# The add that joins the cosine and sine parts of rotary queries and keys: on GpSimd instead of VectorE

## The chip, the cores and the metric

The kernel runs on one core of one Trainium2 chip. The metric is the device time of one execution in microseconds (us). Its engines are TensorE (PE in the profile; PEld is its weight load), VectorE (DVE), ScalarE (ACT), GpSimd (POOL) and SyncE (SP), which starts transfers. Each engine runs its own instructions in program order and waits for the others through counting semaphores.

## The reference

Sixteen sequences of 512 tokens with 512 channels pass through an attention layer and a feed-forward layer. Each layer is wrapped in two layer norms and a residual: `x + layernorm(layer(layernorm(x)))`. What matters here is the attention layer's rotary embedding:

```
q = split_heads(hidden_states @ Wq.T + bq)
k = split_heads(hidden_states @ Wk.T + bk)
apply_rope(x, freqs) = x * cos(freqs) + rotate_half(x) * sin(freqs)
...
scores = einsum('bhqd,bhkd->bhqk', q, k) / sqrt(dh)
weights = softmax(where(causal, scores, -inf))
out = einsum('bhqk,bhkd->bhqd', weights, v)
```

There are 32 heads of 16 channels. The two rotations of the reference (by position and by frame) are one rotation by the summed angle in the kernel's tables.

## The kernel before, in words

The program has two phases: attention for all 16 sequences, then the feed-forward layer for all 16. The change lies in the attention phase. Sequence 0 and the last are written out; sequences 1 to 14 are a loop on every engine.

A sequence is a hand-written order over steps `w`. There are 64 steps (`w` = 0 to 63) that each make one unit of transposed scores on TensorE and its exponentials on ScalarE. Ahead of them lie 16 steps that finish the sequence before. In `w` = 51 to 61 and after the last step each engine also does the **front** of the next sequence: it transposes the normalised input, then projects keys and queries. A front has eight **tiles** `n`, each of 128 tokens by 512 channels: 0 to 3 are keys, 4 to 7 queries. The steps of tile `n` are:

- TensorE projects it into one of two banks of `narrow` (twelve 128x512 matmuls, lines 793 to 795).
- VectorE, `bias_and_cosine` (from line 581): **bias(n)** adds the bias, from PSUM to `biased` (L586), which frees the bank; **cosine(n)** multiplies by the cosine table into `roped` (L590).
- GpSimd, `turn_pairs` (from line 346): two **products** of the swapped halves of `biased` with the sine table, into `turned` (L354 and L356).
- VectorE, `add_sine` (L596): **add(n)**, `roped` = `roped` + `turned`.
- ScalarE, `high_of_k_or_q` (L426): **high(n)** writes the 16-bit high part into `ks` or `qs`.
- VectorE, `low_of_k_or_q` (L603): **low(n)** writes what the high part leaves over.

VectorE's `front` takes them in a staggered order: bias and cosine of `n`, low part of `n - 2`, add of `n - 1`. ScalarE does high(n) two steps after the projection, behind that step's exponentials. `biased` and `turned` have two buffers, `roped` has three. The next sequence's first transposes of queries wait for all eight low parts.

GpSimd has one more duty in these steps. Each key tile of each group of four heads is masked on its diagonal: **mask(k)** (L366, `k` = 0 to 31), in every even step, ahead of that step's `turn_pairs`. TensorE's **weigh(k)** (L896), which multiplies probabilities and values, waits for mask(k). The last ones stand behind the step loop. On GpSimd the order there is tile 6, mask(31), tile 7; on TensorE it is weigh(29), the projection of tile 7, weigh(30), weigh(31), the first parts of the output projection (`project_out`), two transposes (kinds `o` and `a`; **a(3)** is the last), and then the next sequence.

The masks, the products and GpSimd's residual adds (L373) are queued on one engine in one order, so a later one of them can't pass an earlier one.

Of the kernel before, what the change touches and what calls it, by code (L numbers as in the profile page):

```python
# [23 lines left out]
ALU = mybir.AluOpType  # L24
# [7 lines left out]
NT = T // P  # L32
# [38 lines left out]
def attention_phase(nc, x, wT, bias, rope_cos, rope_sin, x1):  # L71
# [5 lines left out]
    with ctx:  # L77
        def sb(name, shape, dt=F32):
            return ctx.enter_context(nc.sbuf_tensor(name, shape, dt))
# [4 lines left out]
        def sem(name):  # L84
            return ctx.enter_context(nc.semaphore(name))
# [30 lines left out]
        turned = sb("turned", [P, 2, C])  # L116
        roped = sb("roped", [P, 3, C])
# [46 lines left out]
        turned_done = sem("turned_done")  # L164
        roped_done = sem("roped_done")
# [134 lines left out]
        @block.sync  # L300
        def _(sp):
            sp.dma_start(xn[:, :, :], x[0, :, :, :]).then_inc(x_in, 16)
            for n in range(4):
                sp.dma_start(probs[:, n, :, :], wT[n]).then_inc(weights_in[n], 16)
            for n in range(4):
                sp.dma_start(bias_sb[:, n, :], bias[n]).then_inc(tables_in, 16)
            sp.dma_start(cos_sb[:, :, :], rope_cos).then_inc(tables_in, 16)
            sp.dma_start(sin_sb[:, :, :], rope_sin).then_inc(tables_in, 16)
            sp.dma_start(xr[:, :, :], x[0, :, :, :]).then_inc(xr_in, 16)

            def sequence(i, last):
                if not last:
                    sp.wait_ge(narrow_full, N_NARROW * i + NC)
                    sp.dma_start(xn[:, :, :], x[i + 1, :, :, :]).then_inc(x_in, 16)
                if not isinstance(i, int) or i > 0:
                    sp.wait_ge(x1_ready, i)
                    sp.dma_start(x1[i - 1, :, :, :], xr[:, :, :]).then_inc(x1_out, 16)
                    sp.wait_ge(x1_out, 16 * i)
                    sp.dma_start(xr[:, :, :], x[i, :, :, :]).then_inc(xr_in, 16)

            sequence(0, False)
            with sp.Fori(1, NB - 1) as i:
                sequence(i, False)
            sequence(NB - 1, True)
            sp.wait_ge(x1_ready, NB)
            sp.dma_start(x1[NB - 1, :, :, :], xr[:, :, :]).then_inc(x1_out, 16)
            sp.wait_ge(x1_out, 16 * NB)

        @block.gpsimd
        def _(pool):  # L330
            nc.gpsimd.memset(ident[:, :], 0.0).then_inc(consts, 1)
            nc.gpsimd.memset(ident16[:, :], 0.0).then_inc(consts, 1)
            nc.gpsimd.memset(causal[:, :], 0.0).then_inc(consts, 1)
            nc.gpsimd.memset(neg_half[:, :], -0.5).then_inc(consts, 1)
            pool.wait_ge(consts, 4)
            for m in (ident, ident16):
                nc.gpsimd.affine_select(out=m[:, :], in_=m[:, :], compare_op=ALU.not_equal, fill=1.0, base=0,
                                        pattern=[[-1, P]], channel_multiplier=1).then_inc(consts, 1)
            tri = causal[:, T - P:T]
            nc.gpsimd.affine_select(out=tri, in_=tri, compare_op=ALU.is_ge, fill=-1e38, base=0,  # L340
                                    pattern=[[-1, P]], channel_multiplier=1).then_inc(consts, 1)
            def inverse_root(i, ready, v, out, done):
                pool.wait_ge(ready, i + 1)
                nc.gpsimd.tensor_tensor(out, v, neg_half[:, :], ALU.pow).then_inc(done, 1)

            def turn_pairs(i, n):

                t = n % NT
                pool.wait_ge(k_and_q_biased, 2 * NT * i + n + 1)
                a = biased[:, n % 2, :].rearrange("p (h d) -> p h d", h=H)  # L350
                o = turned[:, n % 2, :].rearrange("p (h d) -> p h d", h=H)
                s = sin_sb[:, t:t + 1, :]
                half = DH // 2
                nc.gpsimd.tensor_tensor(o[:, :, 0:half], a[:, :, half:DH],  # L354
                                        s[:, :, 0:half].broadcast_to([P, H, half]), ALU.mult)
                nc.gpsimd.tensor_tensor(o[:, :, half:DH], a[:, :, 0:half],  # L356
                                        s[:, :, half:DH].broadcast_to([P, H, half]), ALU.mult).then_inc(turned_done, 1)

            def mask(i, n):

                kt = n % NT
                exps_done = held(pool, NS * i + 2 * n + 2)
                pool.wait_ge(consts, 7)
                pool.wait_ge(st_read, exps_done)
                d = probs[:, kt, :, P * kt:P * kt + P]
                nc.gpsimd.affine_select(out=d, in_=d, compare_op=ALU.is_ge, fill=0.0, base=0,  # L366
                                        pattern=[[0, HG], [1, P]], channel_multiplier=-1).then_inc(masked, 1)

            def residual(i, t):
                if t == 0:  # L370
                    pool.wait_ge(xr_in, 16 * (i + 1))
                pool.wait_ge(projected_normed, NT * i + t + 1)
                added = nc.gpsimd.tensor_tensor(xr[:, t, :], xr[:, t, :], attn[:, t, :], ALU.add)  # L373
                if t == NT - 1:
                    added.then_inc(x1_ready, 1)

            def sequence(i, last):
                for w in range(2, NS + 1):
                    if w == PROJECTED_AT[NT + 1] + 1 and (not isinstance(i, int) or i > 0):
                        inverse_root(i - 1, var1_ready, var1[:, :], rstd1[:, :], rstd1_ready)  # L380
                    if (not isinstance(i, int) or i > 0) and w in RESIDUAL_AT:
                        residual(i - 1, RESIDUAL_AT.index(w))
                    if w % 2 == 0:
                        mask(i, w // 2 - 1)
                    if not last and w == VARIANCE_AT + 3:
                        inverse_root(i + 1, var_ready, var[:, :], rstd[:, :], rstd_ready)
                    n = w - FRONT_AT - NC - 1
                    if not last and 0 <= n < FRONT_SLOTS - NC:
                        turn_pairs(i + 1, n)
                if not last:  # L390
                    for n in range(FRONT_SLOTS - NC, 2 * NT):
                        turn_pairs(i + 1, n)

            inverse_root(0, var_ready, var[:, :], rstd[:, :], rstd_ready)

            for operand in (ks, qs, vs):
                nc.gpsimd.memset(operand[:, :, :, :], 0.0).then_inc(padding, 1)
            pool.wait_ge(padding, 3)
            nc.gpsimd.memset(ks[:, :, :, 3 * DH:3 * DH + 2], SHIFT_UNIT).then_inc(padding, 1)
            nc.gpsimd.memset(vs[:, :, :, DH:DH + 1], 1.0).then_inc(padding, 1)  # L400
            pool.wait_ge(largest_ready, 1)
            nc.gpsimd.partition_all_reduce(largest_all[:, :], largest[:, 0:4], P, RMAX).then_inc(largest_reduced, 1)
            for n in range(2 * NT):
                turn_pairs(0, n)
            sequence(0, False)
            with pool.Fori(1, NB - 1) as i:
                sequence(i, False)
            sequence(NB - 1, True)
            inverse_root(NB - 1, var1_ready, var1[:, :], rstd1[:, :], rstd1_ready)
            for t in range(NT):  # L410
                residual(NB - 1, t)
# [85 lines left out]
        def _(dve):  # L497
# [93 lines left out]
                                        cos_sb[:, t:t + 1, :].broadcast_to([P, H, DH]),  # L591
                                        ALU.mult).then_inc(k_and_q_biased, 1)

            def add_sine(i, n):
                dve.wait_ge(turned_done, 2 * NT * i + n + 1)
                nc.vector.tensor_tensor(roped[:, n % 3, :], roped[:, n % 3, :], turned[:, n % 2, :],  # L596
                                        ALU.add).then_inc(roped_done, 1)

            def low_of_k_or_q(i, n):
                t = n % NT  # L600
                dst, at = (ks, 2 * DH) if n < NT else (qs, DH)
# [5 lines left out]
            def front(i, f):  # L607

                n = f - NC
                if 1 <= f <= NC:  # L610
                    low_of_x(i, f - 1)
                if n < 0:
                    return
                if n < 2 * NT:
                    bias_and_cosine(i, n)
                if n >= 2:
                    low_of_k_or_q(i, n - 2)
                if n == NT:

                    nc.vector.memset(qs[:, :, :, 3 * DH:3 * DH + 2], 0.0)  # L620
                if 1 <= n <= 2 * NT:
                    add_sine(i, n - 1)

            def bias_v(i, t):
                dve.wait_ge(v_full, NT * i + t + 1)
# [782 lines left out]
```

## Time and profile before

| | us |
|---|---|
| runs shown, median (lowest to highest of three) | 3414.96 (3407.57 to 3424.21) |
| the profiled execution, span from first to last instruction | 3413.7 |
| TensorE busy | 2990.8 |
| VectorE busy | 2466.5 |
| ScalarE busy | 1692.8 |
| GpSimd busy | 759.4 |

The page gives the profiled execution by its span. A busy time includes time in which an instruction has been started and is held up, so an operation that looks long may have been waiting. In a row of the timeline the first number is the start in us from the span's start, the second the duration; in brackets stands the idle time before it and what ended it. A wait that ends for several reasons is put down to the last.

### The profile page before, as it was taken

The page shows a single profiled execution, that of the slowest core. Times are in us where ns is not written, and L with a number is a line of the kernel's source. Part 1 is how long each engine was busy: PE and PEld are TensorE (multiplying, and loading weights), DVE is VectorE, ACT ScalarE, POOL GpSimd, SP SyncE. Part 2 cuts the span into 40 slices and gives each one's busy share as a digit, 9 for nine tenths or more (in the row PEclk, how much of TensorE's full clock was granted, in tenths as well). Part 3 has the DMA queues.
Part 4 walks back from the last instruction along what each step waited for, and adds up shares of the span by engine and source line. Part 5 has one row for each costly group of instructions (what it writes and reads, how often), then busy time and mean ns, then how long its engine had stood idle before and what let it go on. Part 6 is the DMA issues. An engine that isn't in the chain of part 4 may idle for free. (4 is left out here: it accounts for less than half of the span.)

```text
span 3413.7 us, 65137 instructions
## 1 busy us (share of the span) xinstructions
PE 2990.8 (88%) x19840; PEld 1439.9 (42%) x19840; DVE 2466.5 (72%) x7030; ACT 1692.8 (50%) x2220; POOL 759.4 (22%) x918
## 2 busy tenths in 40 slices
PE   3798998988889888888888888897299999999998
PEld 1344444444444444444444444443144444444443
DVE  8778778787887878878788787885655545455554
ACT  1647475574755647566475664755322222222222
POOL 3132332323323223332233322332000000000000
PEclk9999999999999999999999999999599999999999
DMA  2000010000100001000010000000311111111110
GB/s 99 1 13 28 12 38 27 14 26 14 38 27 14 26 14 38 26 14 26 14 38 26 14 26 14 26 26 14 142 38 49 61 49 55 44 51 60 49 61 37
DMA packets 16419, 118.72 MB, mean 35 GB/s; under 512 B 2304, under 2 KB 2304, under 8 KB 2944
## 3 DMA queue, kind: packets, MB, share of 16 engines
q1 hardware_dynamic: 16128, 114.90, 8.9%
q8 instruction: 175, 2.87, 0.4%
q14 instruction: 116, 0.95, 0.1%
HBM read 81.34 MB, written 33.55 MB: 34 GB/s over the span
## 5 line engine op out<-in xcount | busy, mean ns | idle before, releaser
L452 ACT ACTIVATE probs<-ring,exp_scale 128x1024 f32<-128x1024 f32 (+3 forms) x1024 | 811.9, 798 | 339.5 <-PE ring L882 334.5
L641 DVE CUSTOM_DVE_ANT_0 narrow<-narrow,causal 128x384 f32<-128x384 f32 (+3 forms) x1760 | 816.6, 487 | 105.8 <-PE narrow L866 102.1
L866 PE MATMUL narrow<-kTz,qT 128*128 128x384 f16 (+3 forms) x1760 | 502.7, 299 | 158.2 <-DVE row_max L641 126.9
L366 POOL TENSOR_SCALAR_AFFINE_SELECT probs<-probs 128x512 f32<-128x512 f32 x512 | 326.6, 638 | 1361.3 <-ACT probs L452 1360.6
L882 PE MATMUL ring<-qmT,kTz 128*128 128x512 f16 (+3 forms) x2048 | 449.3, 301 | 1.7 <-ACT probs L452 1.0
L1262 DVE SCALAR_TENSOR_TENSOR hidden<-gu,up_scale,silu 128x512 f32<-128x512 f32 x176 | 132.0, 750 | 419.2 <-PE gu L1312 419.2
L1121 ACT ACTIVATE silu<-gu,gate_scale 128x512 f32<-128x512 f32 x176 | 121.0, 688 | 632.2 <-PE gu L1312 632.2
L866 PEld LDWEIGHTS narrow<-kTz,qT 128*128 128x128 f16 x1760 | 170.8, 97 | 545.8 <-DVE row_max L641 459.4
L896 PE MATMUL av<-probs,vs 128*32 128x512 f32 (+3 forms) x4096 | 379.3, 445 | 1.4 <-ACT oT L457 0.6
L1310 PE MATMUL gu<-f_xT_hi,gate_hi 128*128 128x512 f16 x704 | 267.9, 381 | 52.1 <-issue 52.1
L641 DVE DVE_READ_ACCUMULATOR2_ANT row_max<- 128x1 f32 x2048 | 284.7, 139 | 0.0
L1312 PE MATMUL gu<-f_xT_lo,gate_hi 128*128 128x512 f16 x704 | 267.8, 380 | 0.0
L1310 PE MATMUL gu<-f_xT_hi,up_hi 128*128 128x512 f16 x704 | 267.6, 380 | 0.0
L1312 PE MATMUL gu<-f_xT_lo,up_hi 128*128 128x512 f16 x704 | 267.6, 380 | 0.0
L1324 PE MATMUL down<-down_hi,hid_hi 128*128 128x512 f16 x704 | 266.8, 379 | 0.2 <-DVE hid_lo L1273 0.2
L1328 PE MATMUL down<-down_hi,hid_lo 128*128 128x512 f16 x704 | 266.8, 379 | 0.0
L1096 POOL TENSOR_TENSOR f_rstd<-f_var,f_neg_half 128x4 f32<-128x4 f32 x32 | 32.3, 1009 | 930.3 <-DVE f_var L1239 647.6
L793 PE MATMUL narrow<-w_hi,xT_hi 128*128 128x512 f16 x512 | 195.6, 382 | 47.5 <-DVE xT_lo L573 47.5
L882 PEld LDWEIGHTS ring<-qmT,kTz 128*128 128x128 f16 x2048 | 180.8, 98 | 85.6 <-issue 24.5
L444 ACT ACTIVATE kTz<-turn 64x1024 f16<-64x1024 f16 x128 | 130.4, 1019 | 152.0 <-PE turn L839 149.7
L444 ACT ACTIVATE qT<-turn 128x1024 f16<-128x1024 f16 x128 | 130.6, 1020 | 131.0 <-PE turn L839 131.0
L794 PE MATMUL narrow<-w_lo,xT_hi 128*128 128x512 f16 x512 | 194.8, 380 | 0.0
(159 smaller groups left out, 5225.7 us busy)
## 6 DMA issues: line engine op xcount, KB each, us to landing
xn<-x SPq DMA_DIRECT2D x16, 1024.0 KB, 4.8
xr<-x SPq DMA_DIRECT2D x16, 1024.0 KB, 4.8
x<-xr SPq DMA_DIRECT2D x16, 1024.0 KB, 3.9
f_xn<-x SPq DMA_DIRECT2D x16, 1024.0 KB, 4.8
f_xr<-x SPq DMA_DIRECT2D x16, 1024.0 KB, 4.8
out<-f_xr SPq DMA_DIRECT2D x16, 1024.0 KB, 3.9
raw_gate<-gateT SPq DMA_DIRECT2D x1, 2816.0 KB, 10.9
raw_up<-upT SPq DMA_DIRECT2D x1, 2816.0 KB, 17.4
```

Of the source, the lines that this page charges most:

```text
L366: nc.gpsimd.affine_select(out=d, in_=d, compare_op=ALU.is_ge, fill=0.0, base=0, pattern=[[0, HG], [1, P]], channel_multiplier=-1).then_inc ...
L444: nc.scalar.activation(dst, src, ACT.Copy).then_inc(turn_read_act, 1)
L452: nc.scalar.activation(probs[:, kt, 2 * pair:2 * pair + 2, P * kt:T], transposed_scores_at(w), ACT.Exp, scale=exp_scale[:, 0:1]).then_inc( ...
L641: nc.vector.tensor_tensor_reduce(out=bank[:, 0:n], in0=bank[:, 0:n], in1=causal[:, T - n:T], scale=1.0, scalar=-3e38, op0=ALU.add, op1=ALU ...
L793: nc.tensor.matmul(out, a_hi, b_hi, start=first, stop=False)
L866: nc.tensor.matmul(bank_of_maximum(2 * s + j)[:, 0:P * (qt + 1)], qT[:, g % 2, pair, P * qt:P * (qt + 1)], kTz[j][:, g % 3, pair, 0:P * (q ...
L882: last = nc.tensor.matmul(transposed_scores_at(w)[:, j, :], kTz[j][:, g % 3, pair, P * kt:P * (kt + 1)], qmT[:, g % 2, pair, P * kt:T], st ...
L896: last = nc.tensor.matmul(av[32 * j:32 * j + 32, P * kt:T], vs[:, kt, HG * g + j, :], probs[:, kt, j, P * kt:T], start=kt == 0, stop=kt == ...
L1310: nc.tensor.matmul(gu[:, bank, :], hi[:, c, cols], xT_hi[:, c, :], start=c == 0, stop=False)
L1312: last = nc.tensor.matmul(gu[:, bank, :], hi[:, c, cols], xT_lo[:, c, :], start=False, stop=end and not with_rest)
L1324: nc.tensor.matmul(down[:, t, :], hid_hi[:, b % 3, rows], down_hi[:, b, :], start=b == 0, stop=False)
L1328: last = nc.tensor.matmul(down[:, t, :], hid_lo[:, b % 3, rows], down_hi[:, b, :], start=False, stop=b == NI - 1)
```

## The change

GpSimd makes the add itself, directly behind the two products of the same tile, and signals `roped_done`; before it, it waits on its own semaphore until the second product has been written. VectorE's `add_sine` and its call are removed.

```diff
@@ turn_pairs, GpSimd
                 nc.gpsimd.tensor_tensor(o[:, :, half:DH], a[:, :, 0:half],
                                         s[:, :, half:DH].broadcast_to([P, H, half]), ALU.mult).then_inc(turned_done, 1)
+                pool.wait_ge(turned_done, 2 * NT * i + n + 1)
+                nc.gpsimd.tensor_tensor(roped[:, n % 3, :], roped[:, n % 3, :], turned[:, n % 2, :],
+                                        ALU.add).then_inc(roped_done, 1)
@@ VectorE
-            def add_sine(i, n):
-                dve.wait_ge(turned_done, 2 * NT * i + n + 1)
-                nc.vector.tensor_tensor(roped[:, n % 3, :], roped[:, n % 3, :], turned[:, n % 2, :],
-                                        ALU.add).then_inc(roped_done, 1)
...
                     nc.vector.memset(qs[:, :, :, 3 * DH:3 * DH + 2], 0.0)
-                if 1 <= n <= 2 * NT:
-                    add_sine(i, n - 1)
```

The order of GpSimd at the end of sequence 0, from tile 5 to tile 7 of the next front, was (the selects are mask(30) and mask(31)):

```order
L354 TENSOR_TENSOR turned<-biased,sin_sb 128x32x8
L356 TENSOR_TENSOR turned<-biased,sin_sb 128x32x8
L366 AFFINE_SELECT probs<-probs 128x4x128
L354 TENSOR_TENSOR turned<-biased,sin_sb 128x32x8
L356 TENSOR_TENSOR turned<-biased,sin_sb 128x32x8
L366 AFFINE_SELECT probs<-probs 128x4x128
L354 TENSOR_TENSOR turned<-biased,sin_sb 128x32x8
L356 TENSOR_TENSOR turned<-biased,sin_sb 128x32x8
```

In the changed kernel the same place reads:

```order
L354 TENSOR_TENSOR turned<-biased,sin_sb 128x32x8
L356 TENSOR_TENSOR turned<-biased,sin_sb 128x32x8
L359 TENSOR_TENSOR roped<-roped,turned 128x512
L369 AFFINE_SELECT probs<-probs 128x4x128
L354 TENSOR_TENSOR turned<-biased,sin_sb 128x32x8
L356 TENSOR_TENSOR turned<-biased,sin_sb 128x32x8
L359 TENSOR_TENSOR roped<-roped,turned 128x512
L369 AFFINE_SELECT probs<-probs 128x4x128
L354 TENSOR_TENSOR turned<-biased,sin_sb 128x32x8
L356 TENSOR_TENSOR turned<-biased,sin_sb 128x32x8
L359 TENSOR_TENSOR roped<-roped,turned 128x512
```

One add now stands ahead of each of the two last masks, and all adds before them stand ahead of both. On VectorE the steps of two tiles in the middle of the same front were (low part, add, bias, cosine, and again):

```order
L603 TENSOR_TENSOR ks<-roped,ks 128x32x16
L596 TENSOR_TENSOR roped<-roped,turned 128x512
L586 TENSOR_TENSOR biased<-narrow,bias_sb 128x512
L590 TENSOR_TENSOR roped<-biased,cos_sb 128x512
L603 TENSOR_TENSOR ks<-roped,ks 128x32x16
L596 TENSOR_TENSOR roped<-roped,turned 128x512
```

and are now:

```order
L601 TENSOR_TENSOR ks<-roped,ks 128x32x16
L589 TENSOR_TENSOR biased<-narrow,bias_sb 128x512
L593 TENSOR_TENSOR roped<-biased,cos_sb 128x512
L601 TENSOR_TENSOR ks<-roped,ks 128x32x16
```

VectorE keeps three steps per tile, in the order they had. TensorE's and ScalarE's orders are as before.

## Rows read from the trace of the kernel before

**Rows 1.** The page, busy us with share of the span and instructions, by engine.

```profile
PE 2990.8 (88%) x19840; PEld 1439.9 (42%) x19840; DVE 2466.5 (72%) x7030; ACT 1692.8 (50%) x2220; POOL 759.4 (22%) x918
```

**Rows 2.** Windows: us, busy PE, PEld, DVE, ACT, POOL, clock, DMA share, GB/s.

```profile
200.00:230.00 30.00, 30.00 (x185) 13.26 (x184) 24.49 (x37) 14.63 (x18) 18.93 (x20) 1.00 0.02 7
```

**Rows 3.** Timeline of VectorE, one front: start, us, instruction, idle time before it.

```profile
495.57 0.69 DVE L596 TENSOR_TENSOR roped<-roped,turned 128x512 f32<-128x512 f32 x1
...
497.26 0.69 DVE L586 TENSOR_TENSOR biased<-narrow,bias_sb 128x512 f32<-128x512 f32 x1 [1.00 <-PE narrow L795]
...
509.38 0.69 DVE L603 TENSOR_TENSOR ks<-roped,ks 128x512 f16<-128x512 f32 x1
509.98 1.21 DVE L596 TENSOR_TENSOR roped<-roped,turned 128x512 f32<-128x512 f32 x1
...
511.83 1.08 DVE L590 TENSOR_TENSOR roped<-biased,cos_sb 128x512 f32<-128x512 f32 x1
...
515.57 0.69 DVE L586 TENSOR_TENSOR biased<-narrow,bias_sb 128x512 f32<-128x512 f32 x1 [0.30 <-PE narrow L795]
```

**Rows 4.** Line 366, the masks: who waited for it (us in all, times).

```profile
  PEld av L896: 8.4, 33
```

**Rows 5.** Timeline of GpSimd, the front before's first product and this front.

```profile
345.47 0.72 POOL L354 TENSOR_TENSOR turned<-biased,sin_sb 128x256 f32<-128x256 f32 x1 [4.02 <-DVE roped L590]
...
491.83 0.72 POOL L354 TENSOR_TENSOR turned<-biased,sin_sb 128x256 f32<-128x256 f32 x1 [4.03 <-DVE roped L590]
...
497.48 0.63 POOL L366 TENSOR_SCALAR_AFFINE_SELECT probs<-probs 128x512 f32<-128x512 f32 x1
...
509.54 1.10 POOL L354 TENSOR_TENSOR turned<-biased,sin_sb 128x256 f32<-128x256 f32 x1 [0.83 <-DVE roped L590]
510.61 1.17 POOL L356 TENSOR_TENSOR turned<-biased,sin_sb 128x256 f32<-128x256 f32 x1
511.74 0.63 POOL L366 TENSOR_SCALAR_AFFINE_SELECT probs<-probs 128x512 f32<-128x512 f32 x1
...
514.06 1.17 POOL L356 TENSOR_TENSOR turned<-biased,sin_sb 128x256 f32<-128x256 f32 x1
515.19 0.63 POOL L366 TENSOR_SCALAR_AFFINE_SELECT probs<-probs 128x512 f32<-128x512 f32 x1
```

**Rows 6.** Timeline of TensorE's weight loads, weigh(31).

```profile
515.87 0.18 PEld L896 LDWEIGHTS av<-probs,vs 128*32 128x32 f32 x8 [0.25 <-POOL probs L366]
```

**Rows 7.** Timeline of TensorE, first matmul of the next sequence in the loop.

```profile
523.34 0.38 PE L793 MATMUL ring<-w_hi,aT_hi 128*128 128x512 f16 x1 [2.15 <-issue]
```

**Rows 8.** Groups by line, VectorE's add: count, busy us, mean ns, idle us before.

```profile
L596 DVE TENSOR_TENSOR roped<-roped,turned 128x512 f32<-128x512 f32 x128 | 135.6, 1059 | 0.0
```

**Rows 9.** Timeline of GpSimd, residual adds of another sequence: a pair, then one alone.

```profile
274.67 2.84 POOL L373 TENSOR_TENSOR xr<-xr,attn 128x512 f32<-128x512 f32 x2
...
278.07 1.27 POOL L373 TENSOR_TENSOR xr<-xr,attn 128x512 f32<-128x512 f32 x1
```

**Rows 10.** Timeline of GpSimd in the set-up: waits on its own semaphores.

```profile
2.15 0.55 POOL L337 TENSOR_SCALAR_AFFINE_SELECT ident<-ident 128x128 f32<-128x128 f32 x2 [0.49 <-POOL neg_half L334]
...
23.66 3.51 POOL L397 MEMSET vs<- 128x4096 f32 x1
27.23 0.48 POOL L399 MEMSET ks<- 128x256 f16 x1
```

**Rows 11.** Timeline of the set-up: first product of tile 0, first transposes of queries.

```profile
67.48 0.72 POOL L354 TENSOR_TENSOR turned<-biased,sin_sb 128x256 f32<-128x256 f32 x1 [21.33 <-DVE roped L590]
...
93.94 1.03 PE L839 MATMUL turn<-ident,qs 128*128 128x128 f16 x8 [9.88 <-DVE qs L603]
```

**Rows 12.** Windows behind the set-up's projections, columns as in rows 2.

```profile
84.00:89.00 5.00, 0.07 (x1) 0.00 (x0) 4.93 (x8) 1.69 (x2) 3.35 (x4) 1.00 0.00 0
89.00:90.00 1.00, 0.00 (x0) 0.00 (x0) 0.65 (x1) 0.31 (x1) 1.00 (x2) 0.61 0.00 0
...
102.00:103.00 1.00, 1.00 (x4) 0.40 (x3) 0.80 (x4) 0.00 (x0) 0.00 (x0) 0.57 0.00 0
```

## The prediction

> **What bounds the kernel now.** I read the busy shares first, to see which engine has no slack: TensorE is busy 88% of the span, GpSimd (POOL) 22% [rows 1]. That is an average, so I went to the stretch where the change acts, the front of the next sequence inside the attention phase. In a 30 us stretch there TensorE is busy 30.00 us, VectorE (DVE) 24.49, GpSimd 18.93 [rows 2]. TensorE sets the pace and VectorE follows it: bias(7) began only when TensorE's projection was done, after 0.30 us of waiting [rows 3]. Freeing VectorE in a stretch that TensorE fills earns nothing by itself.
>
> Next I looked for where TensorE waits for GpSimd. Over the whole run it is 8.4 us in 33 waits [rows 4], which looks like nothing. The place matters, though. At the end of a sequence TensorE runs weigh(30) and weigh(31), each needing its mask. mask(31) starts at 515.19, takes 0.63 and ends at 515.82 [rows 5]; weigh(31)'s weight load starts at 515.87, and its wait was ended by that mask [rows 6]. So **mask(31) has no slack at all**, and it is already queued on GpSimd right behind the products of tile 6, which start at 514.06 and take 1.17 [rows 5]. Behind weigh(31) TensorE goes on without a gap through project_out and the transposes to the sequence's end; then come 2.15 us of issue time at the loop's branch and the next sequence [rows 7]. Every microsecond that mask(31) slips is a microsecond per sequence.
>
> **What the change removes.** 128 adds on VectorE, 135.6 us, 1059 ns on average [rows 8]. Alone such an add takes 0.69 (the first one of this front, 495.57); inside the stretch it takes 1.21 [rows 3], since it waits for GpSimd, as shown next. VectorE's three other steps keep their durations or get longer, and its cosine is ready no earlier where TensorE's projection is what it waits for. I cost this removal at 0: what covers it is TensorE's own work, 30.00 of 30 us.
>
> **How the two engines share.** A product alone takes 0.72 (491.83); beside VectorE 1.10 or 1.17 [rows 5]. Take tile 5: low(3) runs on VectorE from 509.38 to 510.07 [rows 3]; the first product is issued at 509.54 and ends at 510.64 [rows 5], which is 0.72 after 509.92, shortly before low(3) ends. add(4), issued at 509.98, ends at 511.19, which is 0.69 after 510.50; the second product, issued at 510.61, ends at 511.78. So an operation of GpSimd and a VectorE operation with both inputs in SBUF take turns: whichever comes second begins about 0.13 before the other's recorded end. The mask does it too: cosine(6), issued at 511.83 beside mask(30), takes 1.08 instead of 0.69 [rows 3, 5]. The bias step, with an input in PSUM, shows no such wait.
>
> **What it adds on GpSimd.** One 128x512 f32 add per tile. The same form stands in the trace as the residual: 1.27 alone, 1.42 each in a pair beside VectorE [rows 9]. I take 1.27, because I add the turns separately. The GPSIMD Engine Reference of the Trainium skill, section on elementwise cycle accounting, gives 2.6 cycles an element at 1.2 GHz; an estimate from that is 1.11 us and a total of about 3455 to 3467, and its advice to leave elementwise work to VectorE speaks against this change. The row of 1.27 decides. The add also waits for the second product through a semaphore of GpSimd's own. The trace has such waits at 0.06 (a memset ending at 27.17, the next at 27.23) and 0.49 (before the select at 2.15) [rows 10]; I take 0.1, as the first is in warmed-up code, and keep both as ends.
>
> **The queue of one sequence, step by step.** Until add(1) GpSimd has gaps and swallows the new work; add(1) ends near 498.5, where mask(28) began at 497.48 before [rows 5]. From there on it is busy without a break:
> - tiles 2 to 6: 0.72 + 0.72 + 0.1 + 1.27, less 0.06 of overlap between instructions, is 2.75 each, five times 13.8 us;
> - masks 28 to 31: 0.60 each with the overlap, 2.4 us;
> - one real gap of 0.6 us, when cosine(3) itself waited for add(2);
> - turns: VectorE runs cosines 2 to 6 and low parts 0 to 5 in this time, eleven operations, each waited out once. Before, such a wait cost 0.38 and 0.45 (1.10 and 1.17 less 0.72); with 0.42 it is 4.6 us.
>
> Sum 21.4 us, so mask(31) ends near 519.9 instead of 515.82. The mask before it slips to about 515.7, only 0.1 beyond what TensorE asks for. TensorE's shift is 519.9 - 515.8, **about 4.0 us per sequence** after rounding. The adds themselves come no later than VectorE needs them: add(7) ends near 522.7, and high(7) in ScalarE's queue stands behind a transpose that has itself slipped to about 525. There are 15 such tails (sequence 15 prepares no successor): 15 x 4.0 = 60 us.
>
> Once, in the set-up, all eight tiles run with nothing else: GpSimd starts at 67.48, TensorE gets its first transposed queries at 93.94 [rows 11]. Now the tiles follow each other at 2.75 plus two turns of 0.42, 3.6 us: 67.5 + 0.6 + 2.75 + 7 x 3.55 = 95.7 less the overlaps, say 95.2, plus high 1.06 and low 0.69 and hand-overs is 97: **3 us**.
>
> Sum: 3413.7 + 60 + 3 = 3477 us. The span of the profiled execution is 1.3 us below the median of the runs shown, 3414.96, so both can be used alike.
>
> **Bounds.** The same queue with the add at 1.27 to 1.42 [rows 9] and the self-wait at 0.06 to 0.49 [rows 10] gives 3.8 to 5.8 us per tail, so 3474 to 3504. Downwards the turns are the unknown: if GpSimd gets the shared path more often than VectorE and loses 0.2 instead of 0.42 each, the tail costs 4.0 - 2.4 = 1.6 us, in all 3413.7 + 24 + 3 = 3441. The range is 3444 to 3506.
>
> **The rivals.**
> - *No turns for the add (not slower).* If the add runs beside VectorE without waits on either side, a tile costs GpSimd 2.75 us and half a mask, about 3.05, against 3.7 from TensorE (bias(2) at 497.26 and bias(7) at 515.57 both waited for it, five tiles apart [rows 3]); no lag builds up, and mask(31) still ends at about 515.8. The point that decides is whether it ends by 515.87. Time 3414 to 3417. For it: the GpSimd share of 22% [rows 1]. Against it: every product and every cosine that met the other engine was held [rows 3, 5]. Advanced Engine Details and Errata of the Trainium skill, section on VectorE performance modes, says GpSimd and two-port VectorE instructions block each other and lists no two-port mode for tensor_tensor; by that alone this rival would hold, and the 1.21 against 0.69 shows that two SBUF inputs are enough. Chance 0.06.
> - *VectorE was the hidden bound (faster).* Before the tail, in tiles 4 to 6, VectorE's rows follow each other without idle time [rows 3]. If TensorE's next bank waited on that chain, an add of 1.06 us would come back in each: 3 x 1.06 x 15 = 48 us, 3366. TensorE's 30.00 of 30 us [rows 2] leaves no room for it. Chance 0.03.
> - *The clock falls in the stall (much slower).* In the set-up TensorE idled from about 84.1; its granted clock was 1.00 until 89 and 0.61 in the microsecond after it, so it fell near 89.2 from 2.4 to 1.2 GHz, and it was back only at about 102.9 [rows 12], nine microseconds after work resumed at 93.94 [rows 11]. That idle time was ten microseconds, the stall forecast here is four, and the 2.15 us at the loop's branch cost no clock; the trace has nothing between. If the clock fell in every tail, up to half of nine microseconds would come on top: 15 x 4.5 = 67 us, about 3545. Chance 0.06.
> - *The change doesn't do what it says* can be left out: the order shows the add moved.
>
> **How the numbers follow.** The forecast has 0.85, most of it inside 3444 to 3506. A measurement of this kernel tells from no change about 0.5%, 17 us, so the line for slower is 3432 and for faster 3398. The forecast and the clock rival are slower (0.91), less 0.01 for very small waits; the first rival is the same (0.06, with that 0.01); the second is faster (0.03).
>
> **What would show it.** Right: in the changed profile mask(31) ends about 4 us after the products of tile 6 would have let it, weigh(31) waits some 3.5 to 4 us for the mask at each of 15 tails (TensorE's wait for the mask grows from 8.4 to about 65 us), the period of a sequence grows from 146.4 (345.47 to 491.83 [rows 5]) to about 150.4 us, the new add takes 1.27 to 1.7 with its turns, and the projections before the tail start at the same distance from each other as now. Wrong: masks on time and a period of 146; or GpSimd on time and TensorE waiting for the low parts at the next sequence's first transposes instead; or a granted clock below 1.00 behind the stall.

## The result and the profile after

The changed kernel took **3518.39 us**, the median of 4 runs (3511.66 to 3526.54), beside 3412.17 for the kernel before in the same series (4 runs, 3407.57 to 3424.21): a ratio of 1.031, 95% interval 1.0283 to 1.0337. The forecast had the direction and missed the size: 3518 lies above its range. Of the 106 us between the two kernels it accounted for 63.

First the queue, since the forecast worked it out instruction by instruction. GpSimd in the changed kernel, from a front's first product to the mask that TensorE waits for; start, us, instruction, idle time before it:

```profile
504.22 0.72 POOL L354 TENSOR_TENSOR turned<-biased,sin_sb 128x256 f32<-128x256 f32 x1 [4.03 <-DVE roped L593]
...
510.83 1.09 POOL L369 TENSOR_SCALAR_AFFINE_SELECT probs<-probs 128x512 f32<-128x512 f32 x1
...
527.28 0.63 POOL L369 TENSOR_SCALAR_AFFINE_SELECT probs<-probs 128x512 f32<-128x512 f32 x1
527.88 0.73 POOL L354 TENSOR_TENSOR turned<-biased,sin_sb 128x256 f32<-128x256 f32 x1
528.56 0.72 POOL L356 TENSOR_TENSOR turned<-biased,sin_sb 128x256 f32<-128x256 f32 x1
529.36 1.59 POOL L359 TENSOR_TENSOR roped<-roped,turned 128x512 f32<-128x512 f32 x1
530.91 1.09 POOL L369 TENSOR_SCALAR_AFFINE_SELECT probs<-probs 128x512 f32<-128x512 f32 x1
```

The front begins 12.39 us later than the one in [rows 5] (504.22 against 491.83), so mask(31) would have ended at 528.21 with the old queue. It ends at 532.00: **3.8 us late**, where the forecast said 4.0. The add begins 0.08 after the second product's end (528.56 + 0.72, then 529.36); 0.1 was taken.

TensorE at the same place, columns alike:

```profile
527.96 0.64 PE L892 MATMUL av<-probs,vs 128*32 128x256 f32 x8
532.05 0.43 PE L892 MATMUL av<-probs,vs 128*32 128x128 f32 x8 [3.45 <-POOL probs L369]
...
539.94 0.38 PE L789 MATMUL ring<-w_hi,aT_hi 128*128 128x512 f16 x1 [2.60 <-issue]
...
540.59 0.63 PE L789 MATMUL ring<-w_hi,aT_hi 128*128 128x512 f16 x1
...
541.87 0.63 PE L789 MATMUL ring<-w_hi,aT_hi 128*128 128x512 f16 x1
...
544.00 0.38 PE L789 MATMUL ring<-w_hi,aT_hi 128*128 128x512 f16 x1
```

weigh(31) waits 3.45 us; the forecast was 3.5 to 4. The wait is not quite all that a tail loses. The first matmul of project_out stands here, in the kernel before and in the changed one:

```profile
516.25 0.39 PE L793 MATMUL ring<-w_hi,aT_hi 128*128 128x512 f16 x1
...
532.41 0.39 PE L789 MATMUL ring<-w_hi,aT_hi 128*128 128x512 f16 x1
```

From the front's first product that is 24.42 and 28.19 us. TensorE goes on 3.77 us later, by the whole shift of the mask; 15 tails make 56.5 us.

But behind the loop's branch (in [rows 7] the same place) a matmul of the same form takes 0.63 instead of 0.38 for 3.4 us. The windows show why; columns as in [rows 2], two more windows being from 30 us later:

```profile
535.00:540.00 5.00, 2.40 (x14) 1.28 (x13) 2.66 (x5) 1.54 (x2) 0.00 (x0) 1.00 0.02 3
540.00:544.00 4.00, 4.00 (x17) 1.99 (x18) 0.00 (x0) 0.00 (x0) 0.00 (x0) 0.57 0.04 8
...
566.00:571.00 5.00, 3.42 (x15) 1.09 (x13) 3.72 (x13) 1.43 (x2) 0.00 (x0) 1.00 0.01 2
571.00:575.00 4.00, 3.11 (x18) 1.94 (x19) 3.43 (x16) 2.90 (x4) 0.63 (x1) 0.57 0.02 4
```

The granted clock is 0.57 in two stretches of four microseconds, that is, 3.4 us at 1.2 GHz and the rest at 2.4. I call such a stretch a **fall**; one that goes on for 6.8 us counts as two. Ahead of the second one TensorE has no idle time longer than this for 18 us:

```profile
564.59 0.39 PE L862 MATMUL narrow<-kTz,qT 128*128 128x512 f16 x1 [0.78 <-DVE row_max L637]
```

At the end of the next sequence the clock falls while TensorE still waits for mask(31), and stays at 1.2 GHz for 6.8 us; the wait and the window:

```profile
682.04 0.66 PE L892 MATMUL av<-probs,vs 128*32 128x128 f32 x8 [3.45 <-POOL probs L369]
```

```profile
680.50:687.30 6.80, 5.25 (x21) 2.41 (x22) 1.00 (x1) 1.54 (x2) 4.13 (x5) 0.50 0.01 2
```

Falls aren't new. The kernel before has them too, with no wait for a mask in front, one inside a sequence (from 406.7 to 413.5, so it counts as two) and one at a loop's branch (at 1096, in 2.40 us of issue time):

```profile
401.00:406.00 5.00, 3.98 (x17) 1.30 (x15) 3.80 (x13) 1.58 (x2) 0.00 (x0) 1.00 0.01 3
406.00:410.00 4.00, 2.96 (x18) 1.86 (x19) 3.61 (x16) 3.28 (x4) 0.63 (x1) 0.58 0.00 0
410.00:414.00 4.00, 4.00 (x24) 2.57 (x23) 3.17 (x17) 2.92 (x5) 0.63 (x1) 0.56 0.00 0
...
1091.00:1096.00 5.00, 3.10 (x19) 1.75 (x17) 3.59 (x7) 2.60 (x3) 1.22 (x2) 1.00 0.03 7
1096.00:1100.00 4.00, 3.50 (x11) 1.33 (x12) 0.40 (x1) 0.00 (x0) 0.00 (x0) 0.57 0.03 8
```

So the period of a sequence shows both parts. In the kernel before the front at 491.83 is followed by these:

```profile
635.01 0.72 POOL L354 TENSOR_TENSOR turned<-biased,sin_sb 128x256 f32<-128x256 f32 x1 [4.03 <-DVE roped L590]
778.14 0.72 POOL L354 TENSOR_TENSOR turned<-biased,sin_sb 128x256 f32<-128x256 f32 x1 [4.03 <-DVE roped L590]
```

That is 143.2 and then 143.1 us, with no fall in either; the 146.4 of [rows 5] held three. After, the next front is here:

```profile
654.22 0.72 POOL L354 TENSOR_TENSOR turned<-biased,sin_sb 128x256 f32<-128x256 f32 x1 [4.03 <-DVE roped L593]
```

It comes 150.0 us after the one at 504.22, with two falls between: 143.2 + 3.77 leaves 3.0, or 1.5 for each fall.

Counted with windows of 1 us through the attention phase (from 110 us on; time lost to the clock, divided by what one fall loses), the profiled execution of the kernel before has **9 falls and that of the changed kernel 40**. What a fall costs on average I took from the profiled executions of experiments 9 and 10, which have the old order (one with some 1.0 us more of set-up): 20 falls in 3428.9 us and 5 in 3408.1, so (3428.9 - 1.0 - 3408.1) / 15 = **1.32 us**. The clock alone would lose 1.7 in 3.4 us; in part of such a stretch TensorE is idle anyway.

Who waited for the masks, changed kernel (line 369, in [rows 4] 8.4 us in all):

```profile
  PEld av L892: 71.4, 48
  PE av L892: 51.7, 15
```

The matmuls' row is new: 15 times 3.45. In the set-up TensorE's first transposes stand 3.2 us later than in [rows 11], and the first front behind it 3.5 later (205.90 against 202.38):

```profile
97.13 1.03 PE L835 MATMUL turn<-ident,qs 128*128 128x128 f16 x8 [11.66 <-DVE qs L601]
```

**The account**: set-up 3.5 + waits 51.7 + 31 further falls x 1.32 = 40.9, in all 96.1. The spans differ by 3509.9 - 3413.7 = 96.2. The fit is closer than its terms are. With the 56.5 us by which project_out comes later in place of the 51.7, 36 us are left for the 31 falls, 1.17 each; the same count gives 1.0 to 1.3 for each further fall in every other changed kernel below. So of these 96 us some 56 are the late mask and 36 to 41 the clock.

The page and the groups by line, beside [rows 1, 8], show who paid with busy time:

```profile
PE 3033.2 (86%) x19840; PEld 1458.7 (42%) x19840; DVE 2431.3 (69%) x6902; ACT 1688.8 (48%) x2220; POOL 906.2 (26%) x1046
```

```profile
L359 POOL TENSOR_TENSOR roped<-roped,turned 128x512 f32<-128x512 f32 x128 | 186.1, 1454 | 10.0
...
L593 DVE TENSOR_TENSOR roped<-biased,cos_sb 128x512 f32<-128x512 f32 x128 | 118.5, 926 | 4.4
L601 DVE TENSOR_TENSOR ks<-roped,ks 128x512 f16<-128x512 f32 x64 | 78.2, 1223 | 0.0
L601 DVE TENSOR_TENSOR qs<-roped,qs 128x512 f16<-128x512 f32 x64 | 70.9, 1107 | 15.2 <-ACT qs L429 15.2
```

VectorE lost 135.6 us of adds and is busy only 35 us less: its cosines and low parts are now held by GpSimd and take 85 us more (their groups before: 94.5, 43.8 and 44.0 us). Where the other 15 come from these groups don't show.

### The profile page after: what moved, and what is told of

The parts are those of the page before. It is cut to its first block and busy times, and to the rows that moved or that the text cites. A ratio compares the mean times of both kernels' runs of the same rounds, so it can differ in the third digit from the quotient of the medians.

```text
span 3509.9 us, 65137 instructions
## 1 busy us (share of the span) xinstructions
PE 3033.2 (86%) x19840; PEld 1458.7 (42%) x19840; DVE 2431.3 (69%) x6902; ACT 1688.8 (48%) x2220; POOL 906.2 (26%) x1046
## 5 line engine op out<-in xcount | busy, mean ns | idle before, releaser
L369 POOL TENSOR_SCALAR_AFFINE_SELECT probs<-probs 128x512 f32<-128x512 f32 x512 | 347.1, 678 | 1405.1 <-ACT probs L455 1404.7
L878 PE MATMUL ring<-qmT,kTz 128*128 128x512 f16 (+3 forms) x2048 | 459.2, 307 | 1.3 <-ACT probs L455 1.0
L892 PE MATMUL av<-probs,vs 128*32 128x512 f32 (+3 forms) x4096 | 383.8, 447 | 53.7 <-POOL probs L369 51.7
```

Source lines behind the costliest of these rows:

```text
L878: last = nc.tensor.matmul(transposed_scores_at(w)[:, j, :], kTz[j][:, g % 3, pair, P * kt:P * (kt + 1)], qmT[:, g % 2, pair, P * kt:T], st ...
L892: last = nc.tensor.matmul(av[32 * j:32 * j + 32, P * kt:T], vs[:, kt, HG * g + j, :], probs[:, kt, j, P * kt:T], start=kt == 0, stop=kt == ...
```

## The experiments

The theories, by the letters that the expectations use. **A**: the late mask(31) is the cause of everything, its wait and the falls that follow the wait. **B**: the wait is one thing, the falls have another cause in the change. **C**: each add on GpSimd costs time, wherever it stands. **D**: what counts for the falls is how long a sequence takes, not that TensorE idles. The median of the kernel before, run beside them, was 3416.01 in the first four, 3415.53 in the next four and 3420.35 in the last three.

**1. The adds stay on GpSimd, the masks go first.** The add of tile 5 moves behind masks 30 and 31.

```
-            def turn_pairs(i, n):
+            def turn_pairs(i, n, split=False):
...
+                if not split:
+                    join(i, n)        # the wait and the add
...
+                    if w % 2 == 0 and (last or w < NS):
                         mask(i, w // 2 - 1)
+                    if not last and w == NS - 2:
+                        mask(i, NS // 2 - 1)
+                        join(i + 1, w - FRONT_AT - NC - 2)
...
+                        turn_pairs(i + 1, n, split=w == NS - 3)
```

> The changed kernel with mask(30) and mask(31) moved ahead of add(5), so that the two last masks no longer stand behind the adds of tiles 5 and 6; nothing else. Theory A (all that the change costs in a tail comes from TensorE waiting for mask(31), the fall of the granted clock after that wait included): the wait at weigh(31) goes, the clock stays at 1.00 in nearly all tails, and only the set-up's 3.5 us and at most 1 us per tail stay: 3415 to 3430. Rival B (the wait costs its own 3.5 us per tail, and the other 3 us per tail come from the new front itself, from two engines that hold each other up): 3518 - 15 x 3.5 = about 3465.

Measured 3436.88, ratio 1.0051 (1.0036 to 1.0066). The mask is on time; GpSimd's timeline and who waited for line 373:

```profile
517.62 0.72 POOL L356 TENSOR_TENSOR turned<-biased,sin_sb 128x256 f32<-128x256 f32 x1
518.29 1.68 POOL L373 TENSOR_SCALAR_AFFINE_SELECT probs<-probs 128x512 f32<-128x512 f32 x2
519.94 1.27 POOL L363 TENSOR_TENSOR roped<-roped,turned 128x512 f32<-128x512 f32 x1
```

```profile
  PEld av L899: 4.5, 18
```

3518 - 3437: 81 us are gone with all 128 adds still on GpSimd, and project_out begins 24.42 us behind the front, as before. B's 3465 is refuted. But 21 us are left beside the kernel before, 7 more than A allowed, and the profile has 25 falls: 16 more x 1.32 = 21.1, plus 2.2 of set-up, is 23.3; the span is 21.7 above.

**2. The adds stay on VectorE, only the mask is late.** From the kernel before, with four small powers on GpSimd ahead of mask(31); experiment 8 has two.

```
+                    if w == NS and not last:
+                        for m in range(4):
+                            nc.gpsimd.tensor_tensor(idle[:, m, :], idle[:, 4, :], neg_half[:, :], ALU.pow)
                     if w % 2 == 0:
```

> The kernel before, with VectorE still making the adds, and four idle GpSimd powers of 128x4 (about 1.0 us each, results unused) put in front of mask(31) in each of the 15 tails. Only the mask is late, by about 3.9 us less the 0.25 that TensorE waits already. Theory A (a wait of this size at weigh(31) costs itself and as much again nearly through the clock): 15 x 3.7 = 56 plus 15 x 3 = 45, about 3510. Rival B (a late mask costs only its own length): 3412 + 56 = about 3468, with the clock as before.

Measured 3520.34, ratio 1.0287 (1.0254 to 1.032). One of the four, and who waited for the masks (line 368):

```profile
529.06 1.00 POOL L387 TENSOR_TENSOR idle<-idle,neg_half 128x4 f32<-128x4 f32 x1
```

```profile
  PEld av L901: 72.6, 36
  PE av L901: 59.8, 15
```

59.8 + 34 further falls x 1.32 (44.9) = 104.7; the span is 107.7 above. **A late mask alone, with not one add moved, does all that the change does, falls included.** With experiment 1 this shows where the change's time comes from.

**3. Only the adds of the key tiles on GpSimd**, those of the query tiles back on VectorE.

```
+                if n >= NT:
+                    return
                 pool.wait_ge(turned_done, 2 * NT * i + n + 1)
...
+                if NT + 1 <= n <= 2 * NT:
+                    add_sine(i, n - 1)
```

> The changed kernel with GpSimd adding only for the key tiles 0 to 3; VectorE adds for the query tiles 4 to 7, as before. (GpSimd waits for product 4 before the products of tile 5, which costs it under 0.2 us.) Theory A (only the queue that is left at mask(31) counts): three tiles without adds let GpSimd catch up, mask(31) comes within 0.5 us of before, 3412 to 3422 with about 2 us of set-up. Rival C (an add on GpSimd costs wherever it stands): half of the loss, about 3465.

Measured 3443.07, ratio 1.0082 (1.0062 to 1.0101), between A and C. The wait for masks is nearly that of before:

```profile
  PEld av L903: 12.2, 34
```

The profile counts 28 falls: 3.8 - 0.2 + 19 x 1.32 = 28.7 against 26.8 measured. Half of the adds cost 3.8 us of waits and no more; the rest is falls. C's 3465 is refuted, and A's "no wait, no falls" is in trouble.

**4. The wait filled with work.** The changed kernel, with eighteen matmuls more between weigh(30) and weigh(31), on a bank that project_out overwrites.

```
-                weigh(i, NG * NT - 1)
...
+                if not last:
+                    for _ in range(2):
+                        for c in EARLY:
+                            three_products(ring[:, 0, :], aT_hi[:, c, 0:P], ...)
+                weigh(i, NG * NT - 1)
```

> The changed kernel, with TensorE kept busy in the wait: 18 extra 128x512 matmuls (two passes of a product that is made again afterwards, results overwritten) between weigh(30) and weigh(31), 18 x 0.216 = 3.9 us, which covers the wait of 3.45 us. Theory A (the second part of the loss is the clock, and the clock falls because TensorE stands still): falls of the granted clock become as rare as before, TensorE's wait at weigh(31) is under 0.3 us, time 3412 + 3.5 + 15 x 4.0 = about 3475. Rival B (the extra 3 us per tail have another source): 3518 + 15 x 0.4 = about 3524.

Measured 3503.78, ratio 1.0253 (1.0235 to 1.027). The wait is gone, and the clock falls at the branch all the same; TensorE's timeline and the windows around it:

```profile
529.70 0.43 PE L892 MATMUL av<-probs,vs 128*32 128x128 f32 x8
...
537.05 0.38 PE L789 MATMUL ring<-w_hi,aT_hi 128*128 128x512 f16 x1 [2.06 <-issue]
```

```profile
530.00:537.00 7.00, 4.99 (x32) 2.64 (x26) 2.38 (x5) 3.08 (x4) 1.82 (x2) 1.00 0.01 2
537.00:542.00 5.00, 4.95 (x22) 2.50 (x23) 0.33 (x2) 0.80 (x1) 0.00 (x0) 0.66 0.03 10
```

30 falls are left of 40. The work takes 15 x 18 x 0.216 = 58.3 (0.216 is the matmuls' spacing in the timeline); with 2.3 of set-up, 4.1 more of mask waits and 21 x 1.32 = 27.7 that makes 92.4, against 91.4. A's 3475 fails: three quarters of the falls come without that idle time.

**5 and 6. No wait, only a longer sequence.** The kernel before with three (nine in the second) matmuls more ahead of project_out, TensorE busy throughout.

```
+                if not last:
+                    for c in (0,):      # experiment 6: for c in EARLY
+                        three_products(ring[:, 0, :], aT_hi[:, c, 0:P], ...)
```

> The kernel before, with three extra 128x512 matmuls (a product that is made again afterwards, so nothing is left out) ahead of project_out in each of the 15 tails: 15 x 3 x 0.216 = 10 us of TensorE work, no wait, GpSimd and VectorE untouched. Theory D (the granted clock falls more often as soon as a sequence takes another time than 143.2 us, whatever the reason; 16 to 20 more falls of 3.4 us, at 1.25 us each): 10 + 20 to 25, so 3442 to 3447. Theory A (more falls need a wait of TensorE or the adds on GpSimd): 3412 + 10 = 3422 to 3426 with as few falls as before.

> The same with nine extra matmuls per tail: 15 x 9 x 0.216 = 29 us of work. Theory D: 29 + 20 to 25, so 3461 to 3467, many falls. Theory A: 3441 to 3445, few falls.

Measured 3442.98, ratio 1.0074 (1.0051 to 1.0098), and 3456.25, ratio 1.0116 (1.0079 to 1.0153). Three matmuls are 15 x 3 x 0.216 = 9.7 us and brought 27, with 30 falls; nine are 29.2 and brought 41, with 18 falls. The first is what D expected, though the account fits it worst: 9.7 + 21 x 1.32 (27.7) = 37.4, and the span is 31.1 above, 1.0 a fall. In the second the smaller number of falls (9 x 1.32 = 11.9, sum 41.1, span 40.0 above) puts it between A and D. More length doesn't mean more falls.

**7. No add at all.** The kernel before without VectorE's adds, ScalarE waiting for the cosines instead; GpSimd's products are made and not used, so the sine part is left out.

```
-                act.wait_ge(roped_done, 2 * NT * i + n + 1)
+                act.wait_ge(k_and_q_biased, 2 * NT * i + n + 1)
...
-                if 1 <= n <= 2 * NT:
-                    add_sine(i, n - 1)
```

> The kernel before without the add on any engine: ScalarE's high part waits for the cosine step alone, so queries and keys keep only their cosine part, and the sine products are made and not used. It shows what taking the add off VectorE is worth alone. If VectorE is covered by TensorE, as forecast: no gain by it, 3400 to 3416 with the falls as before. Rival (VectorE was the hidden bound): 45 us or more faster. Theory D allows up to 25 us more only if the length of a sequence changes.

Measured 3421.85, ratio 1.0017 (0.9998 to 1.0036). Only the set-up is shorter; the first transposes stand here, against 93.94 in [rows 11]:

```profile
88.34 0.72 PE L837 MATMUL turn<-ident,qs 128*128 128x128 f16 x8 [4.44 <-DVE qs L603]
```

The first front behind it comes 8.0 us earlier (194.41 against 202.38). This is eaten by 16 further falls (21.1; sum 13.1, measured 9.6). In a sequence nothing is gained: project_out begins 24.42 us behind the front, as before. **All 135.6 us of VectorE's adds could vanish and the kernel would not be faster.** The cover that the forecast named holds.

**8. Half the lateness**: two powers instead of four.

> The kernel before with two idle GpSimd powers in front of mask(31) instead of four, so the mask is 2.0 us late and TensorE waits 1.9 to 2.1 us more. Theory A (a fall of the clock follows a long wait): little more than 15 x 2.0 = 30 us, 3446 with few falls. Theory D (falls come with any change of length): 30 + 20 to 25, so 3462 to 3468. Straight from the four-power run, one half of its 104 us: 3468.

Measured 3473.89, ratio 1.016 (1.0124 to 1.0195), above every expectation. Who waited:

```profile
  PEld av L901: 42.8, 35
  PE av L901: 30.6, 15
```

30.6 + 24 x 1.32 (31.7), less 2.1 of a shorter set-up, is 60.2; the span is 62.0 above. Half the wait, 2.0 us, keeps two thirds or more of the falls (33 in all).

**9, 10 and 11. How steady is the number of falls?** The kernel before and the changed one again as they are (9 and 11), and the kernel before with one memset more in the set-up (10).

```
+        setup(nc.vector.memset(w_lo[:, 0, :, :], 0.0))
```

> The kernel before, unchanged, for a second profile: are its nine falls of the clock in the attention phase typical? Theory D needs that: 5 to 14 falls, 3410 to 3420. If the first profile was a lucky one: 20 or more, a span above 3430.

> The kernel before with one more step in the set-up alone (VectorE clears one part of w_lo before it is written; about 1 us once), so that every sequence starts about 1 us later and is otherwise the same. Theory D1 (the number of falls depends on how long a sequence takes): 5 to 14 falls as before, 3413 to 3418. Theory D2 (it depends on when the first sequence starts): another number by 8 or more, and 10 us or more of difference.

> The changed kernel, unchanged, for a second profile: 35 to 45 falls and a span of 3510 if its number is its own; 25 or fewer and under 3495 if it varies from execution to execution as much as between the variants.

Measured 3419.26, ratio 1.0 (0.9983 to 1.0017); 3418.76, ratio 1.0 (0.9988 to 1.0013); 3521.81, ratio 1.0307 (1.0278 to 1.0336). Spans and mean granted clocks of the profiled executions, in this order:

```profile
core 0: 3408.1 us, clock 0.981
```

```profile
core 0: 3428.9 us, clock 0.975
```

```profile
core 0: 3511.1 us, clock 0.963
```

They hold 5, 20 and 44 falls. By its profile alone 10 would speak for D2. But ten runs of each give 9 and 10 the same mean clock, 0.978 and 0.979, and the same time: the 20 are that one execution's. A single profile of this kernel says its number of falls to within some ten.

So I made the account again from every run's mean clock. In 41 runs of the kernel before the mean is 0.978, and (1 - clock) x span averages 76.3 us; in 8 runs of the changed one 0.961 and 137.7. A fall loses half of 3.4 us, so 61.4 us more is 36 falls, 36 to 47 us at 1.0 to 1.3 each. The mean times are 3417.8 and 3519.8, 102.0 apart; less 56.5 for the tails and 3.5 for the set-up that leaves **42** for the clock.

The 36 is an estimate, because a mean clock also counts low stretches that cost no time. The profiled executions of 1, 3 and 4 have one in the set-up, of 27 to 31 us; experiment 1 and the changed kernel, the same window:

```profile
36.00:67.00 31.00, 5.95 (x15) 2.21 (x16) 24.71 (x28) 3.90 (x2) 0.39 (x1) 0.50 0.04 17
...
36.00:67.00 31.00, 5.80 (x16) 2.15 (x17) 24.83 (x28) 3.90 (x2) 0.39 (x1) 1.00 0.06 25
```

A run with such a stretch seems to have eight or nine falls more, and the records of the runs without a profile don't tell which have one.

| kernel | median us | TensorE's new wait (matmuls) | falls in the profile | of these at that wait |
|---|---|---|---|---|
| before | 3412 to 3420 | none | 9, 5 | 0, 0 |
| 10, set-up later | 3419 | none | 20 | 0 |
| 7, no add | 3422 | none | 25 | 0 |
| 1, masks first | 3437 | none | 25 | 0 |
| 5, three matmuls more | 3443 | none | 30 | 0 |
| 3, key tiles only | 3443 | none | 28 | 0 |
| 6, nine matmuls more | 3456 | none | 18 | 0 |
| 8, half the lateness | 3474 | 30.6 | 33 | 11 |
| 4, wait filled | 3504 | none, 58.3 of work | 30 | 0 |
| after | 3518 to 3522 | 51.7 | 40, 44 | 14, 15 |
| 2, only a late mask | 3520 | 59.8 | 43 | 22 |

The last column counts the falls that begin 26 to 30 us behind the front's first product, which is in the wait for mask(31) or within 2 us behind its end, as the one at 680.5 above. No profile without the wait has a fall there, and experiment 4, which fills the wait, has none either. So these falls come with the wait. The largest other group begins 60 to 70 us behind the front's first product, inside the next sequence, as the one at 571: 17 and 20 in the changed kernel, 13 to 16 in experiments 1, 3, 4, 5, 7 and 8, 9 in 2, 4 in 6, against 2, 1 and 8 in the three executions with the old order. For these no experiment shows the cause.

None of these kernels beats the kernel before, and nothing pointed to a version that would.

## Why the prediction was right in direction and too low

- **What bounds the kernel**: right. TensorE fills the attention phase, and experiment 7 puts the worth of VectorE's adds at nothing. The rival of VectorE as the hidden bound is refuted by it.
- **mask(31) has no slack**: right, and shown from both sides. Experiment 2 makes the mask late and nothing else, and gets 3520; experiment 1 makes it punctual with the adds still on GpSimd, and gets 3437.
- **The two engines take turns**: right. VectorE's low part takes 1.76 at worst instead of 0.69 and the add 1.26 to 1.71, so the rival in which the add runs beside VectorE without waits is refuted. The Trainium skill (Advanced Engine Details and Errata, VectorE performance modes) names two-port VectorE instructions and GpSimd as blocking each other and lists no two-port mode for tensor_tensor; taken alone it would have let the add run free, and the measurement decides against that. Nor does the estimate of 1.11 us for an add, from the 2.6 cycles an element of the Trainium skill (GPSIMD Engine Reference, elementwise cycle accounting), show: the shortest of the 128 takes 1.26.
- **The queue**: right to a fraction of a microsecond. mask(31) 3.8 late against 4.0, a wait of 3.45 against 3.5 to 4. The tails' term is 56.5 instead of 60 (3.77 each instead of 4.0); the set-up's is 3.5, and 2.0 in the second profile of the changed kernel, instead of 3.
- **The step that failed is the clock.** The sum priced it at 0. The forecast had it only as a rival with a chance of 0.06 and up to 67 us, worked out from the one long idle time of the set-up [rows 12], and it argued that "the 2.15 us at the loop's branch cost no clock". That was read at one sequence's end. The trace before has falls at other sequences' ends, such as the one at 1096, and it has them inside a sequence, as at 406. Of the signs that it named for being wrong the last, "a granted clock below 1.00 behind the stall", came true. The clock's price is 36 to 41 us in the profiled execution and 42 over all runs. It is more than the whole error: the span is 33 us above 3477, since the tails came 3.5 us cheaper.
- **The range** left the clock out too. Its bounds, worked out as 3441 and 3504, became 3444 to 3506 without a reason; 3518 lies above either.
- **The period**: I forecast 150.4 from 146.4, and 150.0 came, which looks like a hit and isn't one. The 146.4 contained three falls. From a clean 143.2 the same 4.0 would have given 147.2, and the miss would have been in sight.
- **Theory A, my explanation after the result**, holds for the place (the late mask) and only in part for the falls. The longest waits go with the most falls (33 with 2.0 us, 40 to 44 with 3.5 to 4), and 11 to 22 of these stand at the wait itself. But 18 to 30 come in changed kernels without any new wait, and filling the wait removes only those that stand at it (30 falls are left).
- **What stays open**: what decides, for a given length and filling of a sequence, how many of the other falls there are. Apart from those at the wait they stand at three places of a sequence in all these kernels (20 to 22 us ahead of the front's first product, 31 to 41 us behind it, where the loop branches, and 60 to 70 us behind it). In the windows of five microseconds shown, TensorE was busy for 2.4 to 4.0 us ahead of such a fall. Which of the places is hit changes from kernel to kernel and from execution to execution. D in its plain form, more length, more falls, does not hold either (30 with three matmuls, 18 with nine).

## What to carry to other kernels

A queue that runs 22% full can still set the end: look for the one instruction in it that another engine asks for within 0.1 us of its being ready, and count what the change puts ahead of that. Before a wait on TensorE is priced by its length, count the stretches at the lower granted clock in the trace before: this kernel had a few, and every change of a sequence's rhythm tried here brought more, at worst some 40 us on top of 56 us of lateness. Take a period as a base only after looking at its clock.

## What was unexpected of the hardware

- In a phase where TensorE is busy about nine tenths, its clock still falls, in 2.40 us at the loop's branch (1096 in the kernel before), behind 2.06 (experiment 4), and inside a sequence with no idle time over 0.8 us shortly before (406 before, 571 after). A low stretch lasts 3.4 us or twice that, and each 3.4 us cost 1.0 to 1.3 us on average; the nine-microsecond return of the set-up [rows 12] was no measure of it.
- Three matmuls more per sequence, 0.65 us of work, cost 1.8 us, and removing 1.06 us of VectorE work per tile brought falls as well. Every variant here that changes a sequence's timing has a lower mean clock over its runs than the kernel before (0.960 to 0.975 against 0.978; one low stretch in the set-up makes 0.004 of that in a run); the rule behind it was not found.
- The shared path of GpSimd and VectorE is paid twice: the add takes 1454 ns on average on GpSimd instead of 1059 on VectorE, and VectorE's cosines and low parts grow by 85 us in all, most of the reason why 135.6 us taken off VectorE made it only 35 us less busy.
